# Gated attention block with routed experts: the router's logits come out of the output projection, and the first 128 rows of each expert out of one-hot products

## The reference, cut to what matters

```python
# x: 2 batches x 512 tokens x 128; context: 2 x 32 x 128; 16 heads of 8; 8 experts, 128 -> 512 -> 128, top 2
q, k, v = layernorm(x) @ Wq.T + bq, ctx @ Wk.T + bk, ctx @ Wv.T + bv
attn = softmax(q @ k.T * 8 ** -0.5) @ v                     # by head
x = x + tanh(g_xattn) * (attn @ Wo.T)
z = layernorm(x)
logits = z @ Wg.T
top, idx = top_k(logits, 2)
gates = softmax(top)                                        # of the two chosen experts
y = sum over the two of gates * (gelu(z @ W1[e] + b1[e]) @ W2[e] + b2[e])
x = x + tanh(g_ffn) * y
```

## Time and profile before

| | |
|---|---|
| median of 3 runs | 143.9 us (143.31 to 146.18) |
| the profiled execution's own time | 144.68 us |
| its span in the profile | 142.9 us |
| busy PE, DVE, ACT, POOL | 103.3, 91.2, 63.5, 69.0 us |
| moved by DMA | 23.55 MB |

### The profile page before, as it was taken

The page is one execution under the profiler, slowest core; times in us unless marked ns, Lnnn a source line. Parts: engine busy times, 40 slices in busy tenths (PEclk is TensorE's granted clock), DMA queues, the critical chain, the costliest instruction groups (busy, mean ns, idle before and its releaser), DMA issues.

```text
span 142.9 us, 2803 instructions
## 1 busy us (share of the span) xinstructions
PE 103.3 (72%) x973; PEld 64.5 (45%) x973; DVE 91.2 (64%) x249; ACT 63.5 (44%) x168; POOL 69.0 (48%) x101
## 2 busy tenths in 40 slices
PE   5999999949575557469992845898999399984000
PEld 2542354215321444043440315888988298963000
DVE  3776777656869997485984000859877745875033
ACT  3115436684378219252200004949887386680000
POOL 7350972029964274885578300055555535555200
PEclk9999995999999755765899599999999999999755
DMA  3589999990000000111012996781136899511273
GB/s 108 142 260 326 333 344 381 379 323 15 2 0 0 0 5 17 41 37 56 22 38 89 360 344 159 275 304 39 41 143 244 281 355 361 211 39 41 58 272 147
DMA packets 16140, 23.55 MB, mean 165 GB/s; under 512 B 1697, under 2 KB 9612, under 8 KB 16126
## 3 DMA queue, kind: packets, MB, share of 16 engines
q1 hardware_dynamic: 13278, 19.58, 40.0%
q0 software_dynamic: 1248, 2.57, 5.6%
q10 hardware_dynamic: 1600, 1.22, 2.8%
HBM read 7.62 MB, written 7.36 MB: 105 GB/s over the span
## 4 chain that ended last, share of the span: by engine, by line
PE 40%; POOL 15%; DVE 15%; DMA 11%; issue 10%; ACT 5%; SPq 1%; POOLq 0%; DVEq 0%; ACTq 0%
PE bank L700 9%; PE bank L698 8%; POOL sent L494 7%; PE bank L699 6%; DMA z_rows<-sent 4%; POOL wall L459 4%; PE bank L909 4%; DMA sent<-rows,slot 2%; DVE xln L1040 2%; DMA p_hi<-made 2%; ACT p L598 2%; POOL raw L456 2%; PE bank L714 2%; DVE p_lo L1104 2%; DMA made<-raw,z_rows 2%
## 5 line engine op out<-in xcount | busy, mean ns | idle before, releaser
L507 POOL DMA_INDIRECT made<-raw,z_rows x23 | 22.4, 973 | 30.6 <-DVE raw L1247 28.7
L909 PE MATMUL bank<-p_hi 128*128 128x512 f16 x71 | 23.7, 494 | 4.7 <-DMA sent<-rows,slot 3.2
L494 POOL DMA_INDIRECT sent<-rows,slot x16 | 17.5, 1096 | 8.6 <-DVE rows L1195 4.4
L598 ACT ACTIVATE p<-bank,spare_raw 128x128 f32<-128x128 f32 x60 | 17.1, 380 | 4.7 <-PE bank L700 4.6
L1236 DVE TENSOR_SCALAR p<-p 128x512 f16<-128x512 f32 x23 | 9.7, 422 | 14.6 <-ACT p L598 14.4
L1238 DVE SCALAR_TENSOR_TENSOR p<-p 128x512 f16<-128x512 f32 x23 | 15.9, 693 | 0.8
L582 ACT COPY raw<-bank 128x512 f16<-128x512 f16 (+1 forms) x12 | 7.0, 579 | 20.7 <-PE bank L865 19.0
L909 PEld LDWEIGHTS bank<-p_hi 128*128 128x128 f16 x71 | 8.0, 120 | 16.8 <-issue 7.3
L1247 DVE TENSOR_SCALAR raw<-bank,z_rows 128x128 f32<-128x128 f32 x23 | 8.0, 348 | 8.2 <-PE bank L700 8.2
L698 PE MATMUL bank<-spare_raw,p 128*128 128x128 f16 x60 | 10.9, 220 | 1.9 <-DVE p L1238 1.4
L456 POOL TENSOR_SCALAR raw<-raw 128x512 f32<-128x512 f32 x8 | 4.9, 619 | 13.6 <-DVE p_lo L1104 13.6
(11 more groups left out here) (213 smaller groups left out, 285.1 us busy)
## 6 DMA issues: line engine op xcount, KB each, us to landing
spare_raw<-wall SPq DMA_DIRECT2D x15, 546.0 KB, 4.5
sent<-z_rows SPq DMA_DIRECT2D x1, 4160.0 KB, 16.4
raw<-L_ffn_W SPq DMA_DIRECT2D x16, 256.0 KB, 5.6
z_rows<-sent SPq DMA_DIRECT2D x15, 65.0 KB, 2.0
z_rows<-sent ACTq DMA_DIRECT2D x4, 130.0 KB, 3.2
x_sb<-x SPq DMA_DIRECT2D x2, 256.0 KB, 2.9
p_hi<-made SPq DMA_DIRECT2D x2, 256.0 KB, 4.0
p_hi<-made ACTq DMA_DIRECT2D x2, 256.0 KB, 4.2
```

The source lines that it names most:

```text
L494: gp.indirect_dma_start(sent, bass.IndirectOffsetOnAxis(ap=slot[:, b, t, k:k + 1], axis=0), rows[:, b, t, k, :], None).then_inc(scattered[ ...
L507: gp.indirect_dma_start(made, bass.IndirectOffsetOnAxis(ap=z_rows[:, n, ID_AT:ID_AT + 1], axis=0), o_blk[:, n, :], None).then_inc(put, 16)
L598: ac.activation(h32[n % 3][:, c, :], up_bank[n % 3][:, c * P:(c + 1) * P], ACT.Gelu, bias=bias, scale=1.0 / W_SCALE).then_inc(gelu_done, 1)
L909: te.matmul(bank[7][:, :], warm[:, 0:P], warm[:, :], start=True, stop=True)
```

## The change

**Router.** Wg is centred (each row less its mean) and Wo.T Wg.T is put as 8 more columns behind the output projection (`DO` = 136 columns). The logits, up to a positive factor per token, are then those columns plus x's own part, which comes from 24 small products during batch one's attention (`logits_of_x`). The transposes of `zln`, `router`, `z_whole` and `read_logits` go. `choose` no longer needs the layernorm; `scale_gap` multiplies the gap of the two logits by rstd.

**Static rows.** Blocks 0 to 7 take their rows from PE: DVE compares each token's rank with 1 to 128 (`place_early`, `place_last`: 16-bit one-hot tiles), and PE multiplies the rows' halves by them (`spread`, 24 products of 512 columns), which leaves z already transposed; ACT and DVE split it (`first_high`, `first_low`). 64 products of 2 columns (`tell`) give the token number of each place, from which `name_lanes` makes the row numbers for POOL's stores. The 16 indirect stores to `sent` stay, now for the spare blocks alone. The four reads on ACT's queue and the four turns go.

**Gates** are no longer in the row: `weigh` writes `w`, `keep_out` is a plain copy, and `finish` multiplies, a tile at a time.

**Spare list** in 8 steps instead of 11. SP issues all seven first weight copies ahead of the rows.

**Splits of the weights** all on POOL: for experts 1 to 5 ACT also writes the scaled copy, so that POOL only subtracts. Batch two's maxima, `p_low`, the splits on ACT and the bias part are in another order. All `stay_warm` behind the attention go (60 products).

```diff
@@ SP
             for j in range(RING):
                 first.append(spare(j))
-                if j < EARLY:
-                    load_spare(j, first[j])
+                load_spare(j, first[j])
             for part, stores in enumerate(SENT):
                 sp.wait_ge(scattered[part], 16 * stores)
             for j in range(RING):
                 spare_rows(j, first[j])
-            for j in range(EARLY, RING):
-                load_spare(j, first[j])
@@ POOL
+            split_weights(0)
             pool.wait_ge(p_lo_done, G)
-            split_weights(0)
-            split_weights(1)
-            split_weights(2, 0)
+            for e in range(1, 5):
+                split_weights(e)
             rstd_of(2)
-            split_weights(2, 1)
-            pool.wait_ge(p_lo_done, 2 * G)
-            split_weights(3)
+            for e in range(5, E):
+                split_weights(e)
...
+            pool.wait_ge(goes_done, 1)
+            for n in range(E):
                 pool.wait_ge(o_kept, n + 1)
-                gp.indirect_dma_start(made, bass.IndirectOffsetOnAxis(ap=z_rows[:, n, ID_AT:ID_AT + 1], axis=0),
+                gp.indirect_dma_start(made, bass.IndirectOffsetOnAxis(ap=goes_to[:, n:n + 1], axis=0),
                                       o_blk[:, n, :], None).then_inc(put, 16)
@@ ACT
             for g in range(1, G):
                 p_high(1, g)
+            ac.copy(wall_e[:, :, B1_AT:B1_AT + 2 * C].bitcast(F32),
+                    smallT[:, R_B1:R_B1 + E * C].rearrange("p (e c) -> p e c", e=E)).then_inc(b1_done, 1)
+            weights_high(5)
+            rows_high(0)
+            weights_high(6)
+            weights_high(7, 0)
+            o_high(1)
             rows_again(0)
+            weights_high(7, 1)
             router_tanh(0)
-            o_high(1)
-            weights_high(5, 1)
-            weights_high(6)
-            weights_high(7)
...
@@ PE
+            def spread(b, t, half):
+
+                pe.wait_ge(rows_done, b + 1)
+                pe.wait_ge(lanes_last[half] if b else lanes_early, t + 1)
+                for h in range(2):
+                    t_ = te.matmul(spread_bank[half][:, :], rows_h[:, b, t, 0, h * D:(h + 1) * D],
+                                   at_lane[b][:, t, half].rearrange("p l e -> p (l e)"),
...
+            def tell(b, half):
...
+                for e in range(half * A, (half + 1) * A):
+                    for t in range(T):
+                        t_ = te.matmul(told_bank[b][:, TOLD_AT + 2 * e:TOLD_AT + 2 * e + 2], at_lane[b][:, t, half, :, e % A],
+                                       tells[:, b, t, e, :], start=(t == 0), stop=(t == T - 1), skip_group_check=True)
...
-            stay_warm(36)
-            pe.wait_ge(scattered[1], 16 * 6)
-            stay_warm(14)
-            turn(0)
+            for t in range(T):
+                for half in range(2):
+                    spread(0, t, half)
+            for t in range(T):
+                spread(1, t, 0)
+            for half in range(2):
+                tell(0, half)
             up(0)
-            turn(1)
             up(1)
+            tell(1, 0)
+            for t in range(T):
+                spread(1, t, 1)
+            tell(1, 1)
@@ DVE
+            def place_early(t):
...
+                wide = [P, 2, P, A]
+                ve.tensor_tensor(at_lane[0][:, t], lane_no[:, :, :].unsqueeze(1).to_broadcast(wide),
+                                 lane_of[:, 0, t, :].rearrange("p (h e) -> p h e", h=2).unsqueeze(2).to_broadcast(wide),
+                                 ALU.is_equal).then_inc(lanes_early, 1)
+
+            def place_last(t, half):
...
+                ve.tensor_tensor(at_lane[1][:, t, half], lane_no[:, :, :],
+                                 lane_of[:, 1, t, half * A:(half + 1) * A].unsqueeze(1).to_broadcast([P, P, A]),
+                                 ALU.is_equal).then_inc(lanes_last[half], 1)
...
             def finish(b, *parts):
 
                 dve.wait_ge(back[b][0], 16)
-                link(ve.tensor_tensor(half_y[b], taken[b][:, 0].rearrange("p t d -> p (t d)"),
-                                      x1[:, b].rearrange("p t d -> p (t d)"), ALU.add))
+                for t in range(T):
+                    i_ = ve.scalar_tensor_tensor(out=half_y[b][:, t], in0=taken[b][:, 0, t], scalar=w[:, b, t, 0:1],
+                                                 in1=x1[:, b, t], op0=ALU.mult, op1=ALU.add)
```

More of the change, by code:

```diff
@@ L1135, in residual, with rows_low @@
+                    ve.tensor_tensor(logits[:, b, tiles], attended(half)[:, :, D:DO], x_logits[:, b, tiles], ALU.add)
                     i_ = stats_of(x1, b, 2 * half, 2 * half + 1)
                 moments_of(b, i_)
[L1138 to L1147 removed]
+            def rows_low(b):
+                dve.wait_ge(rows_high_done, b + 1)
```

510 lines of the change are left out of this document (314 added, 196 removed).

## The result

The changed kernel takes 154.16 us, median of four runs (153.01 to 156.23), against 143.92 for the kernel before beside it. The ratio is 1.07, with a 95% interval of 1.061 to 1.079: **slower by 7%**, where 6% faster was forecast and 131.5 to 139.5 us was the range. The profiled execution took 156.23 us with a span of 154.5. Executions of one kernel fall into a faster and a slower state; ratios here compare the faster ones alone, and where those were too few, only the median of all is given.

What follows compares the result with a forecast made beforehand. Bound: the wait for POOL's stores to `sent` and the reads before the expert phase, then the PE-led blocks. Block 8 10.1 us earlier, sums 0.9 longer, net -9.2: 134.7 us against 143.9, range 131.5 to 139.5.

Steps and rivals of the forecast that it cites:

- I take 12.8 (11 to 15): Time on PE from `up(0)` at 76.5 to the first turn of spare rows, put at 89.3 us.
- the 5.6: Time from the first turn of spare rows until block 8 is done, at full clock: 5.6 us, ending at 94.9.
- path A: Static rows through DVE and PE, letting blocks 0 to 7 start early; PE reaches the first spare turn at 89.3 us.
- the 12.1: In the kernel before, first expert product (87.29) to the place of the first spare turn (99.4): 12.1 us.
- 9.4 us from 31.2: ACT's weight copies, bias part and `o_high` ahead of `max_rows(1)`: 9.4 us from about 31.2, so it starts near 40.9.
- Stores at 58.3: POOL's stores to `sent` begin at 58.3 us, against 55.26 before: 3.0 us later.
- 4 x 1.83 = 7.3: POOL's splits of experts 6 and 7, with a scaling each, ahead of its stores: 7.3 us from 51.0.
- SP's seven copies: SP's seven register loads and weight copy issues once the spare list is ready: 11.1 us, from 73.4 to 84.5.
- 11.6 forecast: From the end of `normalise` at 64.9 us to `up(0)` at 76.5 us.
- the 0.9 forecast: Sums in `finish` at the end, four ops of 128 instead of one of 512: 0.9 us longer.
- the forecast's 26.3: From the eighth weight copy, which follows block 8, to the last block: 26.3 us, moving as a whole, unchanged.
- Rival 3: PE stays at 1.2 GHz through the expert phase: 150.5 us, or 144.5 if the clock returns earlier; chance 0.05.

Runs made afterwards that it cites:

- e11: Changed kernel with `name_lanes` moved forward on DVE, behind `split_hidden(2)`, so stores to `made` start earlier; 141.3 us against 141.3 for the kernel before.
- e12: Changed kernel with the edits of e1, e3 and e11 together; 143.6 us against 141.3 for the kernel before, ratio 1.027.
- e13: Changed kernel itself once more, nothing edited, on chip 0; 154.8 us against 146.8 for the kernel before, ratio 1.073.
- e16: Changed kernel with e12's edits and the splits of experts 6 and 7 behind all stores on POOL; 141.5 us against 142.2 for the kernel before.
- e1: Changed kernel with the seven early weight copies issued after the loads of the spares' rows; 151.8 us against 146.2 for the kernel before, ratio 1.032.
- e3: Changed kernel with 32 filler products of 512 columns put back on PE; 152.3 us against 146.2 for the kernel before, ratio 1.045.
- e15: Changed kernel with the edits of e3 and e11; 149.3 us against 146.8 for the kernel before, ratio 1.037.
- e14: The program of e11 once more, on chip 0; 152.3 us against 146.8 for the kernel before, ratio 1.042.
- e9: Kernel before, its 36 fillers of 512 columns replaced by 144 of 128; 140.9 us against 141.3 for the kernel before unedited.
- e5: Changed kernel with all 64 products of `tell` and the lane naming moved behind the fourth block; 152.0 us against 144.8 for the kernel before, ratio 1.055.
- e2: Changed kernel with `tell(0)` ahead of batch two's `spread` products instead of behind them; 157.3 us against 146.2 for the kernel before.
- the hold: PE held with fillers until all 16 stores to `sent` have landed; on the changed kernel alone 148.5 us against 141.3 for the kernel before.

## Why the prediction was wrong

**The step that failed** is "I take 12.8 (11 to 15)" for the way from `up(0)` to the spare turn and the 5.6 behind it. Together they were 18.4 and measured 33.0. The sum was not far off as a sum of work: on chip 9, in e11, `up(0)` to the ninth block took 19.8 (e12 21.6), and the kernel before needed 18.7 for the same way. Of the 13 us between 19.8 and 33.0 the two crawls are some 10 (7 and 3), and the half clock behind them is most of the rest: `spread(1, ., 1)` took 3.58 us for 8 products instead of the 1.89 of e11. (These 8 belong to the 32 `spread` products; the 24 that the section on the change names are those ahead of `up(0)`.) Nothing in the profile before shows a crawl: there PE runs little but fillers beside the stores, for which no engine waits. The change put products with consumers there. The prediction put the slowing of PE in this stretch at nothing, without a reason. That the work of an engine may slow down when it is moved beside another's was weighed for DVE and POOL, and not for PE. What makes the crawl stays open.

Two slips in the working changed little. The 5.6 is 7 times 0.75 with 0.4, but the list ahead of it has eight halves of blocks, which makes 6.4; path A's sum stays, since the 5.6 was first taken off the way before (to get the 12.1) and then added again. And 9.4 us from 31.2 is 40.6, not 40.9.

**Stores at 58.3** were at 65.7, and at 60.1 to 65.7 in the other profiles with the changed kernel's splits. This is the 6.4 at `up(0)`: `normalise` ended at 71.8 for 64.9, and the way from there took 0.5 less than forecast. e13, whose attention kept its clock, shows the terms. ACT was nearly as forecast: `max_rows(1)` at 39.83 for 40.9, expert 5 from 48.0 to 50.2 for 47.6 to 49.8. POOL then waited:

```profile
49.28 2.27 POOL L495 TENSOR_TENSOR wall<-raw,wall 128x512 f16<-128x512 f32 x2 [6.36 <-ACT raw L569]
52.97 0.62 POOL L491 TENSOR_SCALAR raw<-raw 128x512 f32<-128x512 f32 x1 [1.42 <-ACT wall L567]
...
54.80 1.06 POOL L491 TENSOR_SCALAR raw<-raw 128x512 f32<-128x512 f32 x1
...
57.06 1.59 POOL L491 TENSOR_SCALAR raw<-raw 128x512 f32<-128x512 f32 x1
```

1.42 us went because ACT's copy for expert 6 is queued behind `rows_high(0)`, and that waits for DVE's `normalise(0)`, which took 2.85 beside POOL instead of 1.28. It ended at 51.63, 0.08 after POOL's two subtractions (49.28 to 51.55), as DVE's small operation in e16 ended with POOL's four. That looks less like a price per piece than like a wait for POOL's splits to end; no run tests it. "4 x 1.83 = 7.3" was 8.7, since two of the scalings took 1.06 and 1.59 beside DVE. With 0.5 more for expert 5 and 0.2 ahead of the first store that is the 3.6 from 58.3 to 61.9, with the attention at full clock up to then. The Trainium skill (GPSIMD Engine Reference, Specifications) says that POOL shares its SBUF interfaces with DVE; the 2.85 and the scalings here agree with that, and I had applied it to the stores only.

**The other 3.8** of the profiled execution are the attention's clock, which I had left as it was. The stretch of the transposed scores, windows as above, first of the changed kernel, then of e13, the same program:

```profile
24.00:31.00 7.00, 7.00 (x15) 1.31 (x13) 4.47 (x10) 3.21 (x6) 2.94 (x4) 0.50 1.06 346
```

```profile
24.00:31.00 7.00, 6.44 (x45) 2.28 (x45) 5.30 (x10) 4.78 (x9) 2.78 (x4) 1.00 1.06 353
```

15 products against 45; 24 of the 45 are the small ones of `logits_of_x`, which the first had not reached. Both waited for ACT's tanh just before. One program can go either way there, by execution. But the change seems to have a share in it: in this stretch the clock was full in 5 of the 15 profiles of the changed kernel and its variants (e1, e3, e12, e13, e15) and at 0.50 to 0.86 in the others, while it was at 0.95 or more in all five of the kernel before and its variants. How large the share is stays open.

**What held.** ACT's work ahead of `max_rows(1)` and batch two's `p_high` (ends 48.0 in e13 for 47.4), tiles of one-hot at 0.69 and 0.42, DVE idle ahead of `normalise` for POOL, the list in 8 steps at 2.1 for 1.9, `tell` at 1.20 for 1.6. From the changed kernel's DVE:

```profile
70.57 1.21 DVE L1127 TENSOR_SCALAR xln<-x,moments,rstd 128x128 f32<-128x128 f32 x4 [3.54 <-POOL rstd L415]
...
72.42 0.69 DVE L1325 TENSOR_TENSOR p_hi<-lane_no,lane_of 128x1024 f16<-128x1024 f16 x1
...
75.53 1.43 DVE L1333 TENSOR_TENSOR p_lo<-lane_no,lane_of 128x512 f16<-128x512 f16 x4
```

SP's seven copies took 11.4 for 11.1. The way from normalise's end to `up(0)`, 11.6 forecast, took 11.1 (71.8 to 82.9). The sums cost more than the 0.9 forecast: from the last block kept to the end it was 13.1, and 11.6 before. From the ninth block kept to the last, 25.3 before, it was 25.7 here, 26.9 in e11 and 25.8 in e12; the forecast's 26.3 is the same stretch counted from the eighth weight copy, and was 25.5 here.

**Rivals.** Rival 3 named the outcome (150.5, slower) and a part of the cause: PE at half clock in slices 13 to 20 and 24 to 25. By e3 against the changed kernel it carries 2.5% and by e15 against e14 0.5%, not the 15.8 us it was priced at, since PE's clock does come back (nine tenths or more in slices 26 to 28), as the argument against it said. Its chance of 0.05 was too low for another reason: all its weight lay on one mechanism, and none on an unknown one between engines whose work had not stood side by side. And without any crawl the forecast would still have missed: e11 and its neighbour before are level at 141.3. There `up(0)` does start 5.5 us sooner than in e9 (81.3 against 86.8) and the ninth block is kept 2.8 sooner (101.1 against 104.0), but the last comes at 128.0 against 127.5, and the sums add their part.

**Open.** What a crawl is. Shown is what it doesn't need: not the copies (e1), not the small products ahead of it (e5), not the half clock (e3), not a fixed product (e1, e2 and e5 crawl in different ones), and not the load alone (e11 beside the changed kernel). A rival that no run tests is PE waiting for its instructions; against it, the queues that fetch instructions moved nothing in the first crawls of the changed kernel, e1, e3, e13, e14 and e15, and in e5 one packet at its start. Shown is that the second crawl went with the edit that names the lanes early (e14, e15 beside e13); that it did so because the stores no longer followed each other is argued. That the first needs POOL's stores is argued from the times of its end alone; the hold that would show it never met a chip that is known to crawl.

## What to carry over

A change that brings the work of two engines together for the first time needs a price for the meeting, not only for the work: here PE's products with consumers, at the end of GpSimd's indirect stores, came 9 us later on one chip than on another, by a cause that stays open, and the profile before could not show it. When "issue" or "remote" fill a hole, look at the engine that waits for the first one's semaphores: if it starts late too, the first one's records end ahead of its signals. Repeat the unchanged kernel on the chip of the variant before crediting an edit: e11 looked like 13 us of gain, and the same program on another chip had none of it.

## What was not expected of the hardware

- The same program spans 150.5 us on one chip and 141.3 on another, and 9.1 of the 9.2 us lie in one stretch, from `up(0)` to the ninth block.
- PE's records can be over 7 us ahead of its signals: the 32 products of `tell(0)` stand as ended at 82.6, and their reader was released at 90.07; in e2 it was 82.53 and 90.19.
- Four `normalise` operations of 128 columns on DVE took 2.85 us beside POOL's splits and 1.21 beside its stores; one operation of 4 columns took 5.25 us in e16, until POOL's splits were done.
- A scaling of 512 columns on POOL took 0.62, 1.06 or 1.59 us, the longer ones beside DVE's operations with two sources (`rows_low`, `b2_low`).
